# Attention over graph edges: TensorE gives a quad's sum signal from a drain behind the products, not from the last product

## What is computed

```python
q = (xn @ wq[l] + bq[l]).reshape(n, H, DH)      # n = 6250, H = 8 heads, DH = 32
k = (xn @ wk[l] + bk[l]).reshape(n, H, DH)
v = (xn @ wv[l] + bv[l]).reshape(n, H, DH)
scores = jnp.einsum('ehd,ehd->eh', q[dst], k[src]) * scale
m = jax.ops.segment_max(scores, dst, num_segments=n)
ex = jnp.exp(scores - m[dst])
z = jax.ops.segment_sum(ex, dst, num_segments=n)
attn = ex / z[dst]
agg = jax.ops.segment_sum(attn[:, :, None] * v[src], dst, num_segments=n)
```

## Time and profile before

| What | us |
|---|---|
| median of three runs | 4993.78 |
| the profiled execution's own time | 4956.99 |
| its span, first to last instruction | 4955.3 |
| PE busy | 3801.7 (77%) |
| DVE busy | 3657.7 (74%) |
| POOL busy | 3311.4 (67%) |
| ACT busy | 2240.1 (45%) |
| mean granted TensorE clock | 0.911 of 2.4 GHz |

### The profile page before, as it was taken

How to read it: one execution, slowest core, us unless ns; L and a number is a source line. 1 busy time by engine, 2 the same in 40 slices (tenths; PEclk the granted TensorE clock), 3 DMA queues, 4 the chain that set the end, 5 groups by cost and what they waited for, 6 DMA issues and landing times. The chain is left out here.

```text
span 4955.3 us, 83612 instructions
## 1 busy us (share of the span) xinstructions
PE 3801.7 (77%) x17590; PEld 2921.6 (59%) x17591; DVE 3657.7 (74%) x9953; ACT 2240.1 (45%) x5559; POOL 3311.4 (67%) x2905
## 2 busy tenths in 40 slices
PE   3686677777777777999986677777777776888879
PEld 1344455555555556888853455555555556778756
DVE  5686688888878886666655688888888886555568
ACT  0122465555556553444411466555555553333322
POOL 2266666666666654888877666666666654888857
PEclk9699899989999998999998899888999998999989
DMA  4577666666666655777766666666666655666668
GB/s 107 177 172 173 196 188 184 186 182 183 180 181 187 179 146 135 158 154 159 152 139 133 199 187 185 183 184 184 184 180 186 178 153 117 135 133 136 130 174 231
DMA packets 683596, 831.56 MB, mean 168 GB/s; under 512 B 147269, under 2 KB 524033, under 8 KB 683301
## 3 DMA queue, kind: packets, MB, share of 16 engines
q0 software_dynamic: 261248, 480.06, 40.0%
q1 hardware_dynamic: 389195, 320.33, 22.3%
q10 hardware_dynamic: 32860, 28.05, 1.9%
HBM read 753.54 MB, written 124.16 MB: 177 GB/s over the span
## 5 line engine op out<-in xcount | busy, mean ns | idle before, releaser
L1042 POOL DMA_INDIRECT kv<-kv_scratch,src_u x1760 | 1775.8, 1009 | 927.0 <-issue 540.1
L1308 PE MATMUL sum_p<-msg,hot_s 128*128 128x273 f32 x3520 | 1128.7, 460 | 541.2 <-DVE sums L1174 383.1
L1308 PEld LDWEIGHTS sum_p<-msg,hot_s 128*128 128x128 f32 x3520 | 704.7, 214 | 850.6 <-DVE sums L1174 396.1
L1514 POOL DMA_INDIRECT sum_scratch<-ysum,dest x600 | 952.6, 1588 | 192.5 <-issue 143.3
L1296 PE MATMUL qe<-sums,hot_q 128*128 x3520 | 909.3, 404 | 99.4 <-ACT hot_q L1064 85.5
L1296 PEld LDWEIGHTS qe<-sums,hot_q 128*128 128x128 f32 x3520 | 718.9, 207 | 245.4 <-issue 117.2
L1174 DVE SCALAR_TENSOR_TENSOR sums<-sums,keep,sum_p 128x273 f32 x880 | 433.8, 493 | 435.5 <-remote 352.0
L1073 ACT ACTIVATE hot_s<-iota_f,ndrel_u 128x128 f32<-128x128 f32 x1760 | 558.4, 391 | 169.2 <-remote 129.9
L1148 DVE TENSOR_TENSOR prod<-qe,kv 128x1024 f32<-128x1024 f32 x440 | 535.6, 1217 | 62.2 <-issue 20.9
L1163 DVE TENSOR_TENSOR msg<-kv,turned 128x1024 f32<-128x1024 f32 x440 | 532.7, 1211 | 6.4 <-issue 6.4
L1155 DVE TENSOR_REDUCE S<-prod 128x32 f32<-128x1024 f32 x440 | 533.9, 1213 | 0.6
(11 more groups left out here) (267 smaller groups left out, 5189.9 us busy)
## 6 DMA issues: line engine op xcount, KB each, us to landing
drow<-drel_scratch SPq DMA_DIRECT2D x220, 256.0 KB
kv<-kv_scratch,src_u POOLq DMA_INDIRECT x1760
ea<-in_edge_attr SPq DMA_DIRECT2D x52, 512.0 KB
srow<-in_src_rows SPq DMA_DIRECT2D x52, 512.0 KB
kv_scratch<-res SPq DMA_DIRECT2D x100, 256.0 KB
ea<-in_edge_attr SPq DMA_DIRECT2D x52, 384.0 KB
srow<-in_src_rows SPq DMA_DIRECT2D x52, 384.0 KB
hin<-h_scratch SPq DMA_DIRECT2D x154, 128.0 KB
```

The lines of the kernel that those rows point to most:

```text
L1042: g.indirect_dma_start(out=kv[:, slot, :], out_offset=None, in_=KVd, in_offset=bass.IndirectOffsetOnAxis(ap=src_u[:, par, u:u + 1], axis=0 ...
L1308: ins = pe.matmul(sum_p[i][:, 0:XW], hot_s[:, q % 2, 2 * i + u, :], msg[:, q % 2, 2 * i + u, :], start=(u == 0), stop=(u == 1))
L1514: g.indirect_dma_start(out=sum_d[r], out_offset=bass.IndirectOffsetOnAxis(ap=dest[:, k, j:j + 1], axis=0), in_=ysum[:, k, j, :], in_offset ...
```

## The change

The signal `sum_s` of a quad is taken off the last matrix product and put on a drain instruction that stands right behind it in TensorE's order. Nothing else changes: the same products in the same order, the same waits, the same number of signals. There is one more TensorE instruction for each of the 440 quads.

```diff
                             for i in range(2):
                                 wait(pe, add_s, c * 2 + i - 1)
                                 for u in range(2):
-                                    ins = pe.matmul(sum_p[i][:, 0:XW], hot_s[:, q % 2, 2 * i + u, :],
+                                    pe.matmul(sum_p[i][:, 0:XW], hot_s[:, q % 2, 2 * i + u, :],
                                                     msg[:, q % 2, 2 * i + u, :], start=(u == 0), stop=(u == 1))
-                            ins.then_inc(sum_s, 1)
+                            pe.drain().then_inc(sum_s, 1)
```

## The result

The changed kernel took 5157.68 us, the median of four runs (5129.23 to 5170.43), against 4992.41 us for the kernel before beside it (four runs; the three of the opening and one more). The ratio is 1.033, with a 95% interval of 1.0305 to 1.0354. The profiled execution has a span of 5168.7 us against 4955.3, so 213.4 us more.

What follows compares the result with a forecast made beforehand. The prediction took VectorE, idling before `add` for held TensorE signals in the attention stages, as the bound. 4957 - 185 = 4772 us, with the median 36.8 us above the profiled execution, gave 4810 us; range 4642 to 5075.

Steps and rivals of the forecast that it cites:

- What bounds the kernel: Attention stages: VectorE is tightest, idling 352.0 us before `add` for TensorE product signals held while GpSimd issues gathers closely.
- does a drain's signal pass while product signals are held?: At `sum_s` behind the sums: yes taken as likeliest, chance 0.44, for a gain of 90 to 350 us.
- the gain of 185 us: Attention stages: middle taken between 156 us of GpSimd's and 215 us of VectorE's unnamed stops, nearer to GpSimd's.
- Rival 1: Behind the sums: drain held too, TensorE stands still, next `spread` moves behind the release; 75 us, so 5069; chance 0.29.
- The number of stops: Before `add`: 116 unnamed stops, a quarter of them (29) priced for the loss.
- The cover: Sums after a moved `spread`: ready at about 1380.6, needed at 1381.1, so covered by 0.5 us at 2.4 GHz.
- The clock: TensorE at 1.2 GHz in a quarter of the stops: sums 2.6 us late, 29 x 2.6 = 75 us.
- The plain price: TensorE behind each quad's sums: a drain costs 0.45 us more, 198 us over 440 quads, covered by TensorE's idling.
- What the profile was to show: Attention stages: if the forecast holds, unnamed idle before `add` under 100 us, stages about 1300 us, drains about 0.4 us.
- Rival 2: Behind the sums: drain held too, but 0.5 us of cover holds nearly everywhere; 4994 within 0.2%; chance 0.15.
- Rival 3: At `products`: drain passes, but late `q_s` and chain signals replace the stops; 4994 or up to 60 us below; chance 0.12.

Runs made afterwards that it cites:

- e1: Kernel before plus a drain without a signal behind each quad's sums, `sum_s` left on the product, on a chip without holds: 1.000 of before.
- e5: The changed kernel as it is, run on a chip without holds: 0.9998 of the kernel before.
- e12: Kernel before plus a drain without a signal behind each quad's sums, `sum_s` left on the product, on a chip with holds: 1.0348 of before.
- e7: Kernel before with `sum_s` moved to the third of the following `spread`'s four `pe.matmul`, no drain, on a chip with holds: 1.0141 of before.
- e9: Kernel before with six extra products into unused columns behind the sums, carrying `sum_s`, no drain, on a chip with holds: 1.0163 of before.
- e6: Kernel before plus a drain without a signal behind each quad's sums, `sum_s` left on the product, on a chip without holds: 0.9998 of before.

## Why the prediction was wrong

**What bounds the kernel: right, on chips of this kind.** Signals of TensorE's products come microseconds late in `attend`, and VectorE loses its time there. The semaphore records of the trace bear it out. In the first attention stage of the kernel before, 272 of the 458 recorded product signals (59%) came over 0.3 us behind their product's end. In the same stage of e1, without holds, none of some 600 did. The signals of VectorE and ScalarE came about 0.01 us behind in either case (6 of VectorE's 955 came over 0.3 us late in the kernel before). These are shares of what was recorded: with holds the trace kept 458 of 604 product signals and 955 of VectorE's 2094, without holds nearly all. That the holds belong to some chips only could not be seen from one trace. One thing in the rows was passed over. The prediction called VectorE, with 1132 us, the tightest engine. But GpSimd's 880 gathers a stage, at a step of 1.31 us, need 1153 us. Without holds they set the pace: in e5 a gather went out every 1.32 us on average, and the stage took 1201 us.

**The step that failed: "does a drain's signal pass while product signals are held?"** I said yes for the likeliest case, and it is no. My argument was that TensorE's queue goes on during a hold, so the engine isn't stuck. But for a drain a product whose signal is held doesn't count as complete: 191 of 440 drains waited 2.8 us on average beyond the last product. e12 settles it, since the drain alone costs 3.5% with the signal where it was, and ends 0.033 us behind that signal. So the gain of 185 us in the forecast's sum wasn't there. The Trainium skill's page "PSUM — Partial Sum Buffer", section "Engine vs sequencer instructions", calls the drain a wait until the engine is fully idle. By the records of this case a held signal keeps TensorE from counting as idle.

**Rival 1 was the right mechanism, with its price too small.** It named the `spread` moved behind the release and asked 75 us. The measured loss is 165 us between the medians and 213 us between the profiled executions, and 5157.68 lies above the range's end of 5075. Its terms were mis-sized in three ways.

- The number of stops. I counted the 116 unnamed ones. In the changed kernel 152 stops stand behind held drains, and 102 more behind drains that ended on time.
- The cover. I gave the late sums 0.5 us of room, worked out from one quad in which VectorE came fresh out of a long stop, and let `scores` and `messages` cover the rest. In e7 and e9 a delay of a good microsecond showed in 187 and 182 stops of about 0.8 us, some 40% of the quads. A line that warned of it was in the trace of before: beside its 116 unnamed stops, `add` also waited 94 times for line 1308 by name, and in 62 of these the signal was on time. There the sums themselves were late, and no room was left.
- The clock. I let a quarter of the stops meet the low clock, and priced each at 2.6 us. With "both parts double", as I wrote, the sums would come at 1384.3 and not at 1383.7, 3.2 us late, which makes 93 us and not 75. In the changed kernel 69 of the 191 held drains (36%) ended at the 1.2 GHz level, and the mean duration of a product of `spread` rose from 404 ns to 461 ns. Products of `spread` that started at the low level were 11% of all before and 27% after. In the windows above it was a long standing still that went ahead of the low clock.

The two traces, one execution each, divide the 211 us of added idling before `add`. Stops in holds, the short named ones counted in, went from 371 to 440 us. Stops for sums that were late with a signal on time went from 36 to 166 us. So the greater part, 130 us, is work pushed back behind the holds, as Rival 1 said. How much of that is the low clock isn't settled. The run meant for it, the drain behind the `spread`, didn't meet a chip with holds.

**The plain price: covered as said, but larger.** 198 us on TensorE were said to be covered. By the 0.60 us measured in e5 it is about 260 us where each drain has a `spread` right behind it. The term that was too small is the one behind the drain: I put 0.2 us for a weight load, and in e5 the next product started 0.41 us (median) after the drain had ended. The changed kernel, the drain behind the sums and the drain behind the `spread` all stand at 1.00 on a chip without holds.

**What the profile was to show.** The prediction said that drains of microseconds where the holds were, no `spread` inside a hold, and an idle time before `add` that doesn't fall would mean Rival 1 or 2. All three are there, and the idle grew by half.

**Rivals 2 and 3.** On a chip without holds the kernel does stand within 0.2%, but not by Rival 2, which spoke of holds that are covered. Rival 3 supposed that the drain passes, and falls with it.

## What to carry to other kernels

Before a signal is moved from the instruction that does the work to a barrier instruction behind it, ask what that barrier waits for. If it waits for the very thing that is late, the engine's other work, which ran during the lateness, is lost on top. Cover should be read from the count of short named stops at the waiting instruction, over all quads, not from one worked example. And an idle time with no named releaser may belong to the chip that the trace was taken on; a second chip is worth more than a tenth run on the first.

## What the runs showed of the hardware

- The same program (the kernel before) took 4570 to 4578 us on one kind of chip and 4962 to 4996 us on the other, 8% to 9% apart. The whole difference lies in the attention stages, where product signals are held on the second kind. From the first gather to the last `add` they took 1395 and 1391 us in the kernel before with holds, and 1198 to 1202 us in runs e1, e5 and e6 without. The rest took 2169 to 2174 us on either.
- A held product signal doesn't stop the next products: in the earlier trace rows eight further products ran while the signal was outstanding. It does stop a drain, and the two are released together (0.033 us apart in e12).
- With holds, in `attend`, they hardly depend on the gathers' bytes (184, 109 or 33 GB/s in the same window gave 352.0, 352.2 and 295.1 us of unnamed idling), and copies on another queue raised it to 531.4 us. In `update`, with closely issued scatters, none of 331 recorded product signals was late.
- Most held drains (134 of 191) ended 1.0 to 1.6 us after GpSimd's last gather had ended.
- Without holds all 440 drains of each run ended 0.02 to 0.05 us behind the last product, with a signal on the drain (e5) nearer to 0.02 and without one (e1, e6) nearer to 0.05.
